# A GRU and a mixture-of-experts layer on one core: x turned by TensorE, biases put into the gate banks by ScalarE, ten input shares computed early

## What is computed

```
for t in range(32):                         # h starts as cond
    gi = x[:, t] @ W_ih + b_ih ;  gh = h @ W_hh + b_hh          # 256 x 768 each
    r, z = sigmoid(i_r + h_r), sigmoid(i_z + h_z)
    n = tanh(i_n + r * h_n)
    h = (1 - z) * n + z * h
xt = all h, as 1024 tokens x 256
probs = softmax(xt @ w_router) ; top 4 of 128, weights normalised
basis = silu(xt @ w_gate) * (xt @ w_up)                          # 8 x 128
mix   = (|amplitudes|^2, normalised)[topk] ; coeff = topk weight * expert_scale[topk]
out   = sum over the 4 of coeff * ((mix . basis) @ w_down)
out  += (silu(xt @ shared_w_gate) * (xt @ shared_w_up)) @ shared_w_down
return x + out
```

## Time and profile before

| what | us |
|---|---|
| median of three runs | 155.8 (155.22 to 156.75) |
| the profiled execution | 155.69 |
| its span | 153.9 |
| TensorE busy | 138.5 (90%) |
| VectorE busy | 112.3 (73%) |
| ScalarE busy | 56.2 (37%) |
| GpSimd busy | 62.6 (41%) |

### The profile page before, as it was taken

The page is one execution under the profiler, slowest core; times in us unless marked ns, Lnnn a source line. Parts: engine busy times, 40 slices in busy tenths (PEclk is TensorE's granted clock), DMA queues, the critical chain, the costliest instruction groups (busy, mean ns, idle before and its releaser), DMA issues.

```text
span 153.9 us, 4173 instructions
## 1 busy us (share of the span) xinstructions
PE 138.5 (90%) x1583; PEld 100.2 (65%) x1583; DVE 112.3 (73%) x417; ACT 56.2 (37%) x190; POOL 62.6 (41%) x116
## 2 busy tenths in 40 slices
PE   7757565998999999999999999999999999998980
PEld 5424343766676777677767876787677776786860
DVE  2063789898789987977697769677967796799750
ACT  0302456463613432343234323432234223433820
POOL 4000236662659343812391139214831465166110
PEclk9975899999999999999999999999999999999998
DMA  4999999200000001000100010000000000000101
GB/s 154 327 227 388 255 200 192 51 0 0 4 2 4 0 0 40 2 4 0 34 4 0 0 34 6 0 4 14 24 0 0 9 31 2 4 0 0 34 8 60
DMA packets 9959, 8.17 MB, mean 53 GB/s; under 512 B 5076, under 2 KB 8404, under 8 KB 9940
## 3 DMA queue, kind: packets, MB, share of 16 engines
q1 hardware_dynamic: 9200, 7.74, 20.9%
q10 hardware_dynamic: 740, 0.17, 0.5%
HBM read 6.86 MB, written 1.05 MB: 51 GB/s over the span
## 4 chain that ended last, share of the span: by engine, by line
PE 73%; DVE 12%; issue 3%; DMA 3%; ACT 2%; ACTq 2%; POOL 1%; DVEq 0%
PE unit L529 32%; PE gates L520 16%; PE gates L507 11%; PE down L594 5%; DMA bh<-in_L_cond_b_hh_dram 3%; PE gates L501 2%; DVE sc_out L739 2%; PE route L541 2%; ACT sc_add L380 1%; ACTq L231 1%; DVE pre L730 1%; PE route L569 1%; DVE p L792 1%; DVE m L727 1%; ACT trz L373 1%
## 5 line engine op out<-in xcount | busy, mean ns | idle before, releaser
L291 POOL CAST hThi<-hT 128x64 fp32r<-128x64 f32 x32 | 8.3, 260 | 74.3 <-DVE hT L746 73.8
L373 ACT ACTIVATE trz<-gates 128x128 f32<-128x128 f32 x32 | 8.9, 279 | 71.8 <-PE gates L520 71.8
L529 PE MATMUL unit<-whi,hThi 128*128 128x512 f32 x80 | 33.8, 422 | 0.8 <-DVE wlo L764 0.6
L520 PE MATMUL gates<-whh,hT 128*32 128x192 f32 x512 | 28.2, 339 | 6.4 <-DVE hT L746 4.8
L529 PE MATMUL unit<-wlo,hThi 128*128 128x512 f32 x80 | 31.6, 395 | 0.0
L529 PE MATMUL unit<-whi,hTlo 128*128 128x512 f32 x80 | 31.5, 394 | 0.0
L507 PE MATMUL gates<-wih,xT 128*32 128x192 f32 x512 | 28.1, 337 | 0.0
L520 PEld LDWEIGHTS gates<-whh,hT 128*32 128x32 f32 x512 | 13.7, 111 | 18.5 <-issue 9.5
L739 DVE TENSOR_TENSOR_SCAN sc_out<-sc_mul,sc_add 128x128 f32<-128x128 f32 x32 | 14.5, 453 | 8.3 <-ACT sc_add L380 8.2
L507 PEld LDWEIGHTS gates<-wih,xT 128*32 128x32 f32 x512 | 16.5, 113 | 4.4 <-issue 0.4
L529 PEld LDWEIGHTS unit<-whi,hThi 128*128 128x128 f32 x80 | 15.1, 189 | 5.9 <-issue 2.9
(11 more groups left out here) (113 smaller groups left out, 213.5 us busy)
## 6 DMA issues: line engine op xcount, KB each, us to landing
wraw<-in_L_ffn_w_gate_dram SPq DMA_DIRECT2D x2, 512.0 KB, 7.1
wraw<-in_L_ffn_w_up_dram SPq DMA_DIRECT2D x2, 512.0 KB, 7.7
xtok<-in_x_dram SPq DMA_DIRECT2D x4, 256.0 KB, 6.9
out_dram<-ot SPq DMA_DIRECT2D x8, 128.0 KB
wih<-in_L_cond_W_ih_dram SPq DMA_DIRECT2D x2, 384.0 KB, 3.8
whh<-in_L_cond_W_hh_dram SPq DMA_DIRECT2D x2, 256.0 KB, 5.3
xj<-in_x_dram SPq DMA_DIRECT2D x4, 128.0 KB, 7.3
xj<-in_x_dram SPq DMA_DIRECT2D x4, 96.0 KB, 5.6
```

The source lines that it names most:

```text
L373: act.activation(trz[:, :], gates[t % 2][:, R:R + 2 * FJ], ACT.Tanh, scale=0.5).then_inc(rz_ready, 1)
L520: last = pe.matmul(g[Q * j:Q * (j + 1), HN:HN + 3 * FJ], st, whh[:, s, :].rearrange("p (g j c) -> p j g c", g=3, j=NJ)[:, j], start=False, ...
L529: last = pe.matmul(dst, st[:, p % 2, s, :, :].rearrange("p t b -> p (t b)"), w[:, s, :, cols], start=(s == 0 and n == 0), stop=(s == KB - ...
```

## The change

x is loaded once, one transfer of 128 KB for each chunk, in the layout of `xtok`. TensorE turns it (`turn_x`, two 128x128 transposes for a chunk into a bank); VectorE copies chunks 0 and 1 out (`keep_x`), ScalarE the others in pairs of 512 columns (`keep_x_pair`, in the slots of steps 0, 1 and 2). The bf16 pieces of the bias and their selection rows are gone. The bias is spread by float32 matmuls three times at the start: into both gate banks for steps 0 and 1, and into `down`, from which ScalarE keeps it in SBUF (`keep_bias`). From step 2 on ScalarE copies it into the gate bank (`load_gates(t + 2)`, first thing of its slot of step t), and `x_part` only adds to the bank. `x_part(0)` and `x_part(1)` stand ahead of the loop. For the ten steps of EARLY the input share is computed during the first chunk (two before step 0, then one, two, two and three in the slots) into banks of the filler; VectorE adds the bias (`keep_early`) and keeps it in `early`; GpSimd fills the HN columns of it; `load_gates` takes it in place of the bias, and `x_part` is left out for these steps. The logits of the first pass wait until all ten are kept.

```diff
+EARLY = [4, 5, 6, 8, 12, 13, 16, 20, 24, 28]
+BEFORE_FIRST = 2
+EARLY_AFTER = [1, 2, 2, 3]
+        early_bank = unit_bank + [turned, down]
-        def load_x(queue, t0, t1, loaded):
-            for j in range(NJ):
-                queue.dma_start(xj[Q * j:Q * (j + 1), t0:t1, :], x[:, t0:t1, FJ * j:FJ * (j + 1)]).then_inc(loaded, 16)
+        def load_x(queue, c):
+            queue.dma_start(xtok[:, c, :], x.rearrange("b (c t) d -> c t b d", t=TC)[c]).then_inc(ld_xtok[c], 16)
...
-            load_x(sp, TC, 4 * TC, ld_x1)
+            for c in range(2, NC):
+                load_x(sp, c)
...
-            load_x(sp, 4 * TC, T, ld_x2)
...
-            for t in range(TC):
-                sp.dma_start(xtok[Q * t:Q * (t + 1), :, :],
-                             x.rearrange("b (c t) d -> t b c d", t=TC)[t]).then_inc(ld_xtok, 16)
...
+            pool.wait_ge(bias_ready, 1)
+            pool.tensor_copy(early[:, :, HN:HN + FJ],
+                             bias[:, HN:HN + FJ].rearrange("p (o c) -> p o c", o=1).to_broadcast([P, NE, FJ]))\
+                .then_inc(early_hn, 1)
...
-            load_x(act, 0, TC, ld_x0)
+            load_x(act, 0)
             for name, dst in ((b_ih, bi4), (b_hh, bh4)):
                 act.dma_start(dst[:, :, :], name.rearrange("(g j c) -> j g c", g=3, j=NJ)).then_inc(ld_bias, 16)
+            load_x(act, 1)
             act.dma_start(h0[:, :], cond.rearrange("b (j c) -> j b c", j=NJ)).then_inc(ld_h0, 16)
 
+            def keep_bias():
+                act.wait_ge(bias_raised, 1)
+                act.activation(bias[:, :], down[:, 0:4 * FJ], ACT.Copy).then_inc(bias_ready, 1)
+
+            def load_gates(t):
...
+                if t in EARLY:
+                    act.wait_ge(early_ready, EARLY.index(t) + 1)
+                act.activation(gates[t % 2][:, 0:4 * FJ], early[:, EARLY.index(t), :] if t in EARLY else bias[:, :],
+                               ACT.Copy).then_inc(gates_loaded, 1)
+
+            def keep_x_pair(c):
+                act.wait_ge(x_raised, c + 2)
+                act.activation(xT[:, c:c + 2, :, :].rearrange("p c s n -> p (c s n)"), route[:, 0:4 * P], ACT.Copy)\
+                    .then_inc(x_pair_turned, 1)
...
+                if TC * c + k + 2 < T:
+                    load_gates(TC * c + k + 2)
                 if c == 0:
+                    if k < 3:
+                        keep_x_pair(2 * k + 2)
                     if k == 1:
                         hi_router()
                         hi_pieces(0, 1)
...
+            def turn_x(c, dst, half):
+                pe.wait_ge(ld_xtok[c], 16)
+                for s in range(KB):
+                    last = pe.transpose(dst[:, 2 * P * half + P * s:2 * P * half + P * (s + 1)],
+                                        xtok[:, c, :].rearrange("p (f s) -> p s f", s=KB)[:, s, :], ident[:, :])
+                last.then_inc(x_raised, 1)
...
-                for j in range(NJ):
-                    which, bias = (pick4[:, j, :], bsum[:, 0, :]) if t == 0 else \
-                        (pick[0:2 * Q + NJ, j, :], bias3[0:2 * Q + NJ, :])
-                    pe.matmul(g[Q * j:Q * (j + 1), 0:4 * FJ], which, bias,
-                              start=True, stop=False, skip_group_check=True)
+                if t < 2 or t % TC == 0 or t - 1 in EARLY:
+                    wait_x(t)
+                if t >= 2:
+                    pe.wait_ge(gates_loaded, t - 1)
...
             def h_part(t):
 
                 pe.wait_ge(hT_ready, t + 1)
+                if t in EARLY:
+                    pe.wait_ge(gates_loaded, t - 1)
...
+                if p < 0:
+                    first = BEFORE_FIRST + sum(EARLY_AFTER[:k])
+                    for n in range(first, first + EARLY_AFTER[k]):
+                        early_x_part(n)
+                    if k < 3:
+                        if k == 0:
+                            pe.wait_ge(x_turned, 2)
+                        else:
+                            pe.wait_ge(x_pair_turned, k)
+                        turn_x(2 * k + 2, route, 0)
+                        turn_x(2 * k + 3, route, 1)
                 if p >= 0:
+                    if k == 0 and p == 0:
+                        pe.wait_ge(early_ready, NE)
...
+            for dst in (down, gates[0], gates[1]):
+                last = spread_bias(dst)
+                if dst is down:
+                    last.then_inc(bias_raised, 1)
+            turn_x(0, route, 0)
+            turn_x(1, unit_bank[2], 0)
             x_part(0)
-            pe.wait_ge(const_ready, 5)
-            pe.wait_ge(bias_step, 11)
+            x_part(1)
+            for n in range(BEFORE_FIRST):
+                early_x_part(n)
             for c in range(NC):
                 for k in range(TC):
                     t = TC * c + k
                     h_part(t)
-                    if t + 1 < T:
+                    if 1 <= t < T - 1 and t + 1 not in EARLY:
                         x_part(t + 1)
                     filler(c, k)
...
+            def keep_early(n):
+                dve.wait_ge(early_raised, n + 1)
+                if n == 0:
+                    dve.wait_ge(bias_ready, 1)
+                dve.tensor_tensor(early[:, n, R:4 * FJ], early_bank[n % len(early_bank)][:, R:4 * FJ],
+                                  bias[:, R:4 * FJ], ALU.add).then_inc(early_ready, 1)
...
-                for n in x_due(c, k):
-                    turn_x(TC * n, TC * (n + 1), ld_x2)
                 if c == 0:
-                    if k == 0:
-                        turn_x(TC, 3 * TC, ld_x1)
+                    first = BEFORE_FIRST + sum(EARLY_AFTER[:k])
+                    for n in range(first, first + EARLY_AFTER[k]):
+                        keep_early(n)
                     if k == 1:
-                        turn_x(3 * TC, 4 * TC, ld_x1)
                         lo_router()
                         lo_piece(0)
```

More of the change, by code:

```diff
@@ L75, in build @@
         bh4 = sb("bh4", [NJ, 3, FJ])
-        bsum = sb("bsum", [NJ, 3, 4 * FJ])
-        bpart = sb("bpart", [NJ, 3, 4 * FJ], BF16)
-        bias3 = sb("bias3", [P, 4 * FJ], BF16)
+        bsum = sb("bsum", [NJ, 4 * FJ])
+        bias = sb("bias", [P, 4 * FJ])
+        early = sb("early", [P, NE, 4 * FJ])
         empty = sb("empty", [P, 2 * P], BF16)
         pick4 = sb("pick4", [NJ, NJ, Q])
-        pick = sb("pick", [P, NJ, Q], BF16)
         ident = sb("ident", [P, P])
@@ L146, in build @@
         ld_h0 = sem("ld_h0")
-        ld_x0 = sem("ld_x0")
-        ld_x1 = sem("ld_x1")
-        ld_x2 = sem("ld_x2")
-        ld_xtok = sem("ld_xtok")
+        ld_xtok = [sem(f"ld_xtok{c}") for c in range(NC)]
         ld_mix = sem("ld_mix")
@@ L163, in build @@
         mix_step = sem("mix_step")
+        x_raised = sem("x_raised")
         x_turned = sem("x_turned")
+        x_pair_turned = sem("x_pair_turned")
+        bias_raised = sem("bias_raised")
+        bias_ready = sem("bias_ready")
+        early_raised = sem("early_raised")
+        early_ready = sem("early_ready")
+        early_hn = sem("early_hn")
+        gates_loaded = sem("gates_loaded")
         w_hi = sem("w_hi")
@@ L219, in by_block, with x_block @@
             return tile[:, :, a].rearrange("p (s c) -> p c s", s=KB)
-        def x_due(c, k):
-            return [n for n in range(4, NC) if (n - 3, 1) == (c, k)]
         def unit_order(p):
             return list(range(NU)) if p < NC - 1 else [NU - 1] + list(range(NU - 1))
-        def load_x(queue, t0, t1, loaded):
-            for j in range(NJ):
-                queue.dma_start(xj[Q * j:Q * (j + 1), t0:t1, :], x[:, t0:t1, FJ * j:FJ * (j + 1)]).then_inc(loaded, 16)
+        def load_x(queue, c):
+            queue.dma_start(xtok[:, c, :], x.rearrange("b (c t) d -> c t b d", t=TC)[c]).then_inc(ld_xtok[c], 16)
+        def x_block(t, s):
+            return xT[:, t // TC, s, B * (t % TC):B * (t % TC + 1)]
         @block.sync
@@ L469, in slot @@
                         hi_down()
+            keep_bias()
             for c in range(NC):
@@ L492, in _, with spread_bias, wait_x @@
         def _(pe):
+            def spread_bias(dst):
+                for j in range(NJ):
+                    last = pe.matmul(dst[Q * j:Q * (j + 1), 0:4 * FJ], pick4[:, j, :], bsum[:, :],
+                                     start=True, stop=True, skip_group_check=True)
+                return last
+            def turn_x(c, dst, half):
[4 more added lines that the diff above has]
+                last.then_inc(x_raised, 1)
+            def wait_x(t):
+                if t // TC < 2:
+                    pe.wait_ge(x_turned, t // TC + 1)
+                else:
+                    pe.wait_ge(x_pair_turned, t // TC // 2)
             def x_part(t):
                 g = gates[t % 2]
-                if t % TC == 0 and t > 0:
-                    pe.wait_ge(x_turned, {1: 2, 2: 2}.get(t // TC, t // TC))
-                for j in range(NJ):
-                    which, bias = (pick4[:, j, :], bsum[:, 0, :]) if t == 0 else \
```

(24 more changed lines are left out.)

58 lines of the change are left out of this document (23 added, 35 removed).

## The result

The changed kernel takes 155.0 us (median of ten, 154.64 to 155.45) against 156.46 of before in the same runs (155.22 to 156.95): the ratio is 0.9915, 95% interval 0.9888 to 0.9941. It is faster by 0.9% where 3.4% was forecast; the prediction itself took a change of 1% as about what can be told from none. The profiled execution has a span of 153.0 instead of 153.9. Of all runs in this document one, the 153.27 of best3w, was a slow one, and the ratios leave it out.

The account below looks back on a forecast made before the run. TensorE alone was taken to bound the kernel from 39.35 to 133.10, with waits for biases, weights and remainders before. 155.7 - 1.25 (start) + 3.2 (first chunk) - 0.8 (given back) - 6.4 (steady) = 150.45, forecast 150.5; range 147.5 to 154.3.

Parts of the forecast that it names:

- The steady stretch: TensorE-bound from 39.35 on: 23 biases of 0.11 (2.5) and six input shares of 0.65 (3.9) go, minus 6.4 us.
- The rival in which skipped steps give nothing: Steady stretch: VectorE or the recurrence becomes the bound in skipped steps, 3.9 us more, 154.3; chance 0.1.
- The first chunk and what is given back: Moved work stretches the first chunk's steps by 3.2 us; the second chunk gives back 0.8.
- ScalarE's wait for the transposes: First chunk, step 1: the x pair's copy waits until 2.5, weight rounding queued behind; m comes 1.35 us later.
- the lock: First chunk, step 2: VectorE's remainder waits for GpSimd's on a common port, 4.15 us; without hindrance 3.45.
- The start: Ahead of the first chunk's step 1 sigmoids: they come at 15.75 instead of 17.01, minus 1.25 us.
- the biases' landing at 6.3: Start: biases issued 1.4 us earlier land at about 6.3; bound 7.65 if they wait for weights in front.
- the spreadings: Start: TensorE spreads the bias over three banks, at most 1.9 us, taken as 1.5 for overlap.
- turns and copy: Start: TensorE's x turns, 0.25 us a pair, and VectorE's copy, 0.41; first input share at 9.25.
- four input shares: Start: shares of steps 0, 1, 4, 5 before the first hidden share, 0.65 us each, ending at 11.85.
- the granted clock: Start: TensorE assumed at full clock (1.00), since it would stand still for only 0.2 and 0.4 us.
- The rival of the falling clock: Start: clock falls at about 9.4 as before, plus 0.7 us instead of minus 1.25, so 152.4; chance 0.25.

Follow-up runs that it names:

- best3w: split_bias with only six early shares, initial state right behind the biases, split_bias_order's ScalarE order, twelve more useless matmuls before x's first turn: 149.94 us, ratio 0.9516.
- no_early: The changed kernel with no input share computed early, the bias still going by ScalarE: 157.29 us, ratio 1.0103 to the kernel before.
- bias_first: The changed kernel with both biases issued ahead of the first chunk's x on ScalarE's queue: 155.57 us, ratio 0.9968 to the kernel before.
- warm40: The changed kernel with 40 instead of 28 warm-up matmuls: 154.31 us, ratio 0.9884 to the kernel before.
- split: The changed kernel with each x load split into four transfers of 32 partitions: 153.8 us, ratio 0.9842 to the kernel before.
- split_bias: The changed kernel with biases first on ScalarE's queue and x in transfers of 32 partitions: 151.66 us, ratio 0.9736 to the kernel before.
- split_bias_order: split_bias with ScalarE rounding router and weight pieces ahead of copying the x pair in steps 1 and 2: 150.12 us, ratio 0.9599 to the kernel before.

## Why the prediction was wrong

**The steady stretch** (minus 6.4): right. It measured minus 6.6; biases 2.8 and six skipped shares 3.8 by no_early. The rival in which skipped steps give nothing is out: the recurrence became the longer one in one place only, at the skipped shares of steps 12 and 13, for 0.1.

**The first chunk and what is given back** (plus 2.4): right, plus 2.53 (3.14 and minus 0.61). ScalarE's wait for the transposes with the queue behind it is shown by the run that puts it last (0.94 in step 1 to 2), the lock by the run that takes it away (0.68). That steps 4, 5, 6 and 8 give nothing is shown too.

**The start** (minus 1.25): this step failed; it was plus 3.17. By its own terms: the biases' landing at 6.3 measured 7.68 (+1.4); the spreadings were 2.6 and not 1.5 (+1.1); turns and copy 1.3 and not 0.85 (+0.4); four input shares 4.15 and not 2.6 (+1.6). The last three are mostly the granted clock, which was taken as full and was 0.50 from 9.3 to about 15.

The landing is where it went wrong first. 7.65 was the bound that I had named and not taken, for a wait behind the weights; bias_first shows that it was x, in front of the biases on the same queue (3.81 when they go first). TensorE then stood still for 2.07 before 8.31, where the prediction had 0.2 and 0.4, and the clock fell; with the rest before the spreadings shortened to 0.78 (warm40) or gone (bias_first) they ran at full clock.

The other thing is the form of the x transfer, which no sentence of the prediction looks at. I took its landing from transfers (5.6 to landing) whose outermost dimension is 32 partitions. The new one has four outermost, and ran on about a quarter of the engines. In the changed kernel TensorE didn't wait for it, because the biases were later still, and on the biases it had little effect: from issue to use they took 5.40 behind the one transfer and 4.79 behind the four of split. But with the biases mended alone, x was the next to be late (11.49), and the gain was gone. With the form and the order mended (split_bias) the same start takes what was forecast, and the profiled execution lands within 0.2 of it; that is in part luck, since the clock didn't fall in that execution, and the median is 1.2 above the forecast.

**The rival of the falling clock** (152.4) had the right mechanism and one quarter of the chance; it assumed that only the clock differs. With the biases late as well it would have been 153.8, and the spreadings at half clock make up the rest.

What stays open is what makes the clock fall or hold around a pause of 0.8 to 1.5 us: split_bias and split_bias_order went opposite ways with the same start, the longer pause keeping it, and best3w, where a part of the pause was filled, still lost it.

## To carry to other kernels

Work that is moved out of a bound stretch lands somewhere; price the landing place as carefully as the gain. Here 6.6 us of gain met 2.5 us in the first chunk and 3.2 us at the start. Only the shares that left the bound stretch paid; four of ten were moved from one place with room to another without.

When transfers are merged, look at the outermost dimension of both sides and at what stands behind them in the same queue: fewer issues can mean fewer engines (a DMA share of 0.27 here). And where several arrivals gate a start, moving one uncovers the next (here biases, second x, weights, initial state in turn), so list all of them with their landings before counting a gain from any.

## Not expected of the hardware

128 KB transfers with four outermost rows ran at a DMA share of 0.27 and some 95 GB/s. Two transfers of 3 KB issued behind x on the same queue were read at 7.68 (8.03 behind x in its split form), and at 3.81 ahead of it. The early sums on VectorE, which read a bank, took no longer while GpSimd worked (two in 0.61 at 26.57, beside GpSimd's splitting of the state), whereas a remainder with both operands in SBUF went from 0.69 to 1.36. That was with GpSimd's started first (1.29 for it); in split_bias_order VectorE's started first, and took 0.69 beside 1.74.
